# Attention with a fused dense layer on one core: the first maxima lead the scores by 32 instead of 48, their relu gets two places per side, and the next rows' statistics stand two by two ahead of two maxima

## The reference

```python
xn = layernorm(x)
q = relu(xn @ Wq.T + bq); k = relu(keys @ Wk.T + bk); v = relu(values @ Wv.T + bv)
# 16 heads of 16 columns
score = einsum('bhsd,bhtd->bhst', qh, kh) / sqrt(16)
attn = softmax(score, axis=-1)
a = transpose(einsum('bhst,bhtd->bhsd', attn, vh), (0, 1, 3, 2)).reshape(...)
w = (weights >= 0) * 2 - 1
y = clip((xn @ w.T) * scale + bias, -100, 100)
out = x + (a + xn) + y
```

## Time and profile before

| | us |
|---|---|
| median of 3 runs (2899.27 to 2910.23) | 2900.64 |
| profiled execution | 2900.54 |
| its span, first to last instruction | 2898.7 |
| TensorE busy, 97% of the span | 2809.6 |
| ScalarE busy, 84% | 2439.8 |
| VectorE busy, 81% | 2341.8 |
| GpSimd busy, 32% | 938.2 |
| mean granted TensorE clock, of full speed | 0.981 |

### The profile page before, as it was taken

The page is one execution under the profiler, slowest core; times in us unless marked ns, Lnnn a source line. Parts: engine busy times, 40 slices in busy tenths (PEclk is TensorE's granted clock), DMA queues, the critical chain, the costliest instruction groups (busy, mean ns, idle before and its releaser), DMA issues.

```text
span 2898.7 us, 61156 instructions
## 1 busy us (share of the span) xinstructions
PE 2809.6 (97%) x17860; PEld 1195.3 (41%) x17860; DVE 2341.8 (81%) x4578; ACT 2439.8 (84%) x2955; POOL 938.2 (32%) x845
## 2 busy tenths in 40 slices
PE   8899999999999999999999999999999999999996
PEld 4444444444444434444444444444444444444331
DVE  6788888888888888888888888888888888888840
ACT  4788888888888888888888888888888888888896
POOL 4304333242343314433242342414333242343001
PEclk8599999999999999999999999999999999999998
DMA  7111111121211111111111211121111121211111
GB/s 140 58 38 55 64 62 35 61 65 58 64 62 50 46 65 58 64 60 37 61 64 58 64 59 49 50 68 54 64 62 35 61 65 57 64 62 36 46 54 38
DMA packets 78637, 167.75 MB, mean 58 GB/s; under 512 B 28547, under 2 KB 32646, under 8 KB 76326
## 3 DMA queue, kind: packets, MB, share of 16 engines
q1 hardware_dynamic: 78374, 164.19, 18.8%
HBM read 36.71 MB, written 17.83 MB: 19 GB/s over the span
## 4 chain that ended last, share of the span: by engine, by line
PE 73%; issue 11%; DVE 7%; ACT 3%; POOL 1%; DVEq 0%; SPq 0%; DMA 0%; ACTq 0%; POOLq 0%
PE value_ps L606 27%; PE ring L628 24%; PE score_ps L592 16%; DVE mx L950 6%; ACT probs L798 3%; PE score_ps L657 1%; PE score_ps L672 1%; PE score_ps L674 1%; PE score_ps L659 1%; PE score_ps L661 1%; POOL fin L1088 1%; DVE stats L975 1%; DVE excess L926 0%; DVEq L945 0%; PE ring L637 0%
## 5 line engine op out<-in xcount | busy, mean ns | idle before, releaser
L798 ACT ACTIVATE probs<-score_ps 128x1024 f32<-128x1024 f32 x2048 | 1996.6, 1027 | 301.0 <-PE score_ps L592 292.6
L950 DVE TENSOR_REDUCE mx<-ring 128x1 f32<-128x512 f32 x2940 | 1894.0, 684 | 348.0 <-PE ring L628 335.3
L628 PE MATMUL ring<-kstack,qstack 48*128 48x512 f32 x3430 | 1125.0, 464 | 11.1 <-DVE mx L950 4.5
L606 PE MATMUL value_ps<-probs,vones 128*32 128x512 f32 x8192 | 1093.3, 606 | 0.8 <-ACT probs L798 0.3
L628 PEld LDWEIGHTS ring<-kstack,qstack 48*128 48x128 f32 x3430 | 525.5, 184 | 948.3 <-DVE mx L950 891.8
L592 PE MATMUL score_ps<-qstack,kstack 51*128 51x512 f32 x4096 | 827.0, 426 | 24.3 <-ACT probs L798 15.5
L592 PEld LDWEIGHTS score_ps<-qstack,kstack 51*128 51x128 f32 x4096 | 414.1, 186 | 262.6 <-ACT probs L798 222.2
L1088 POOL TENSOR_TENSOR dense<-dense,affine 128x512 f32<-128x512 f32 x128 | 164.1, 1282 | 869.6 <-ACT dense L848 868.2
L926 DVE CUSTOM_DVE_ANT_0 excess<-ring,excess 128x512 f32<-128x512 f32 x534 | 369.2, 691 | 78.0 <-PE ring L628 49.9
L814 ACT ACTIVATE excess<-ring 128x512 f32<-128x512 f32 x490 | 293.9, 600 | 7.6 <-PE ring L628 4.4
L606 PEld LDWEIGHTS value_ps<-probs,vones 128*32 128x32 f32 x8192 | 161.5, 108 | 288.3 <-issue 276.6
(11 more groups left out here) (93 smaller groups left out, 1437.0 us busy)
## 6 DMA issues: line engine op xcount, KB each, us to landing
qstack<-parts SPq DMA_DIRECT2D x768, 64.0 KB, 2.5
fin<-taken SPq DMA_DIRECT2D x256, 128.0 KB, 2.9
xin<-x SPq DMA_DIRECT2D x16, 1024.0 KB, 4.9
base_cur<-base_new SPq DMA_DIRECT2D x16, 1024.0 KB, 5.4
fin<-recip SPq DMA_DIRECT2D x32, 512.0 KB
out<-fin SPq DMA_DIRECT2D x32, 512.0 KB, 2.6
qstack<-proj SPq DMA_DIRECT2D x256, 12.0 KB
kstack<-base_cur SPq DMA_DIRECT2D x16, 128.0 KB, 6.2
```

What stands on the lines that cost most here:

```text
L606: mm = pe.matmul(value_ps[h4 * 32:(h4 + 1) * 32, :], vones[:, 2 * tp + c, hh * HALF + side * PAIRS + 2 * g + j, :, :], probs[:, q % 2 * GR ...
L628: pe.matmul(ps[:, :], qstack[nh][rows, pair, st * P:(st + 1) * P], keys, start=True, stop=True).then_inc(s_mm, 1)
L798: nc.scalar.activation(probs[:, q % 2 * GROUP + u % GROUP, :], score_ps[src][:, :], ACT.Exp, scale=EXP_SCALE).then_inc(s_probs, 1)
L950: nc.vector.tensor_reduce(most, src[:, :], AX.X, ALU.max).then_inc(s_mx, 1)
```

## The change

`LEAD` goes from 48 to 32. The start has 40 steps instead of 44. In each pass the next half's maxima, and the splits with them, begin at duo 24 instead of 20, and `ROWS_DUO` goes from 22 to 26. The relu of the start has two places for each side, chosen by the parity of the step, and waits for the join of the step before the last. The start's statistics stand in steps 35 to 38, its aggregates behind step 39, which is now the last. In the passes the statistics stand in the duos 15, 17, 19 and 21, one ahead of maximum 3 and one ahead of maximum 6 of the octet. On SyncE gather 2 stands ahead of the load of the rows.

```diff
-        start_excess = [excess[:, :], probs[:, 4, 0:BANK]]
+        start_excess = [[excess[:, :], probs[:, 4, 0:BANK]], [probs[:, 5, k * BANK:(k + 1) * BANK] for k in range(2)]]
...
-        LEAD = 48
-        ROWS_DUO = 22
+        LEAD = 32
+        ROWS_DUO = 26
         RECIP_UNIT = 14
         AGGREGATE_DUO = 23
+
+        STATS_DUOS, STATS_AHEAD = (15, 17, 19, 21), (3, 6)
...
-        START_STATS = FIRST_ROWS + 5
-        assert START_ROWS < len(START)
+        START_STATS = FIRST_ROWS + 3
+        assert max(START_ROWS, START_STATS + 4) < len(START)
...
+                if att:
+                    gather(*att, 2)
                 if now:
                     load_rows(b, hh)
-                if att:
-                    gather(*att, 2)
...
             def take_start_differences(j):
                 for side in range(SIDES):
-                    wait(act, s_mx, 2 * (j - 1) + side + 1)
+                    wait(act, s_mx, 2 * (j - 2) + side + 1)
                     act.wait_ge(s_mm, 2 * SIDES * j + side + 1)
-                    nc.scalar.activation(start_excess[side], score_ps[j % 2][:, side * BANK:(side + 1) * BANK],
+                    nc.scalar.activation(start_excess[j % 2][side], score_ps[j % 2][:, side * BANK:(side + 1) * BANK],
...
-                    join(ring[at[side]][:, :], start_excess[side], mx[:, hh, st, h, 1:2])
+                    join(ring[at[side]][:, :], start_excess[j % 2][side], mx[:, hh, st, h, 1:2])
...
                         for n in itertools.chain(*maxima_of(d)):
+                            if prep and d in STATS_DUOS and n % 8 in STATS_AHEAD:
+                                statistics(b, *ROW_TILES[2 * STATS_DUOS.index(d) + STATS_AHEAD.index(n % 8)])
                             reduce_bank(b, hh, n, at)
...
-                    if prep and AGGREGATE_DUO - 8 <= d < AGGREGATE_DUO:
-                        statistics(b, *ROW_TILES[d - AGGREGATE_DUO + 8])
```

## The result

| | before | changed kernel |
|---|---|---|
| median, us | 2901.32 (20 runs, 2897.91 to 2910.23) | 2913.36 (20 runs, 2906.0 to 2926.04) |
| ratio, 95% interval | | 1.0038 [1.0029, 1.0048] |
| profiled execution / its span, us | 2900.5 / 2898.7 | 2911.5 / 2909.7 |
| mean granted TensorE clock | 0.981 | 0.978 |

The forecast was 2880 us, its range 2869 to 2891. The kernel became slower, clear of the interval but by less than the 0.5% that the prediction named as its bound for a change.

What follows compares the result with a forecast made beforehand. TensorE and VectorE were taken to hold each other in the long middle, with VectorE idling in gaps. From 2900.5 us: start -9.5, last pass +1.8, statistics -10.2, queries -3.4, rows +1 gave 2880 us, range 2869 to 2891.

Steps and rivals of the forecast that it cites:

- The start, -9.5 us: Before the first pass: steps go from 1.50 to 1.24 us, GpSimd's root starts at 106.1 for 116.13; -9.5 us.
- Rival (a): In the start: steps stay in the relu and join loop, giving -3.8 for -9.5, total 2886 us; chance 0.14.
- The last pass, +1.8: Last pass with maxima: duos 20 to 23 get maxima and take 9.8 us for 8.0; +1.8 us.
- The statistics, -10.2: In 14 hh=0 passes: moved statistics use VectorE's gaps, their extra 1.43 us becomes 0.7; -10.2 us.
- The 0.1 us a pair: hh=0 passes: allowance for a 0.33 us statistic exceeding the gap ahead of the join; 0.4 us over the pairs.
- Rival (b): In passes with statistics: the statistics keep their price, term 0, total 2890 us; chance 0.15.
- rival (c): In hh=0 passes: statistics and aggregates become free, 1.43 becomes 0.2, 7 us less, total 2873 us; chance 0.12.
- the 1.43: Extra us six pairs take in hh=0 over hh=1, for statistics, aggregates and their effect on the maxima's splits.
- The flush: On VectorE: a 0.42 us statistic would hold the engine about 0.57 us, making the statistics term 0, sum about 2890.
- The queries, -3.4: Next half's queries: one 1.75 us TensorE wait and the 3.4 us at half clock after it go; -3.4 us.
- The rows, +1: Rows turned at duo 26 in 31 passes: ScalarE's copy near the sums and splits costs 0.03 us each; +1 us.
- rival (d): Rows' load lands too late for the next pass's scores, margin 2.2 us; 2926 us if held 3.7 us; chance 0.04.

Runs made afterwards that it cites:

- experiment 1: Changed kernel with 32 waiting instructions ahead of TensorE's first work, putting its loop head back at 1750: 2867.95 us, ratio to before 0.9887.
- experiment 7: Kernel before with only the statistics of the passes moved, loop head staying at 1750: 2889.47 us, ratio 0.9960.
- experiments 11 and 12: Kernel of experiment 1 with 18 waiting instructions more on ScalarE, then also 24 on VectorE: 2871.72 us and 2873.67 us.
- experiment 9: Kernel before with only the two relu places per side in the start: 2888.33 us, ratio 0.9962.
- experiment 2: Kernel before with 224 waiting instructions ahead of TensorE's first work, loop head at 1974: 2963.94 us, ratio 1.0215.
- experiment 3: Changed kernel with the same 32 waiting instructions put behind the last pass instead: 2913.95 us, ratio to before 1.0046.

## Why the prediction was wrong, step by step

- **The start, -9.5 us:** right. Pass 1 begins 9.5 us earlier in the changed kernel and 10.2 in the kernel of experiment 1; root at 105.97, predicted 106.1; steps of 1.22 us, predicted 1.24. That root is what counts holds: the first exponential came 12.0 us earlier, and 2.5 us of that were given back in pass 0, in the stall on the normalised rows. Rival (a) fell.
- **The last pass, +1.8:** measured +1.5. The four duos take 9.9 us with their maxima, predicted 9.8, for 8.00:

```profile
2794.25:2804.15 9.90, 9.83 (x67) 3.77 (x63) 9.13 (x17) 8.61 (x12) 0.00 (x0) 1.00 0.00 0
```

- **The statistics, -10.2:** direction right, too small. In the kernel without stops a pass with hh = 0 is 1.07 us shorter, -15 us for 14 passes. Alone the statistics give -0.76 (experiment 7) and the lead -0.08. The 0.1 us a pair that I kept for a statistic in a gap of 0.24 is not there, the pairs take 4.88 us. The last 0.2 us comes only with both moves together; that it lies in the splits beside the aggregates is not shown. Rival (b) fell, and rival (c) was nearer than the forecast: it left 0.2 us of the 1.43, the runs 0.36. The flush that the prediction sets against this term is not in the changed kernel either: the join starts 0.33 us after a statistic of 0.41 (430.67). The section of the Trainium skill that the prediction cites for it (VectorE: DVE Perf Modes, the DRAIN you can't avoid) also says that a next operation that is not held starts earlier, which the prediction leaves out: so the section does not speak against this term as the prediction has it.
- **The queries, -3.4:** right in the mechanism, and in the size by luck of the execution. Pass 10 is 3.3 us shorter, but it is so too in the three other traces with a lead of 48. One of these, experiment 9's, has a wait of 1.66 us in pass 26 and one of 0.47 in pass 30, one (experiment 7's) a wait of 0.40 in pass 30, and one (experiment 2's) 0.13 in pass 30. No trace with the lead of 32 has any. So the wait is an event that moves and can be absent, and by those three traces the term is worth some 2 us or less.
- **The rows, +1, and rival (d):** nothing. The load is issued from 453.69 for 6.05 us, 6.18 in the earlier trace rows, and TensorE's first scores of the next pass wait for no DMA. The passes with hh = 1, which carry the move as well, are as long as before (in the median 85.49 before, 85.45 changed), and 85.37 in experiment 1.
- **What failed** is the step that dealt with the four steps taken out of the start. The prediction said that they come back at the end for +1.8 us, and it costed them as time only: VectorE's joins at one end, two pairs of duos at the other. They are also 32 instructions of TensorE's program, and the sum had no term for where the program's loop then lies. That missing term is +41 us: 13 stops of 1.9 to 2.5 us, and five stretches at half clock. None of the four rivals contained it. The prediction's own test, "the forecast is wrong as a whole if the hh=1 passes lengthen", looked at the wrong half: these have no jump ahead of them.
- **A second missing term**, -3.9 us in pass 29, has the same nature on ScalarE and VectorE (experiments 11 and 12). The kernel before has its other stretch at half clock there, 3.4 us from 2691.0, behind ScalarE's stop; the prediction, which named the one in pass 10 only, did not see it.
- With these terms the sum comes out: 2880.2, less 0.3 for the last pass, 4.4 for the statistics (14 x 1.04 beside 10.2, against the 87.06 from which the stops are counted), 1.3 for the rows and 3.9 in pass 29, plus 0.1 for the queries and 41.0 for the stops, is 2911.4, for 2911.5 in the profiled execution.
- **Without the stops** the forecast would have been 12 us too high: experiment 1 measured 2867.95, just under the range. What it missed there is 4.8 us of the statistics, 4.3 in pass 29 and 2.4 in the passes with hh = 1, where the rows were to cost 1 us and the time fell by 1.4; the rest is in small parts.

The version to keep is the kernel of experiment 1: the whole change, with the head of TensorE's loop where it was. It is 1.1% faster than the kernel before, and its runs lie within 0.35 us of each other where those of before spread over 12.

## What to carry to other kernels

An edit ahead of a loop moves the loop in every engine's program, and a loop whose head lay 16 or fewer instructions ahead of a block's border (one such distance was tried) paid some 2 us at each jump here, and often the clock after it; one whose head lay some 50 ahead paid too. Before believing the verdict on such an edit, compare the packets of the instruction queues on the two pages (172 and 185 here) and look for "issue" waits of 2 us in the middle of runs of equal instructions. If they are there, move the head by some waiting instructions and time again: the ratio of this change turned from 1.0038 [1.0029, 1.0048] to 0.9887 [0.9872, 0.9903].

## What the runs showed of the hardware

- TensorE's program comes in packets of 16384 bytes; a block that came behind a jump had landed 2.2 to 2.8 us after the branch (at 550.18: packet at +1.2 us, 1.2 us long), and the next matmul started only 1.2 to 1.5 us later (554.03 for 552.6); what these are stays open. The hint saves 3.7 us of idle time at a jump (4.10 - 0.39), and covers one block.
- ScalarE's and VectorE's come in packets of 8192 bytes, and the first pass behind a loop cost ScalarE a stop of 2.15 us and VectorE one of 2.20 us in two kernels that differ from a third only by 18 and 24 instructions that do nothing.
- A stop of TensorE of 2 us was followed by the half clock five times of 13 in the changed kernel, four in experiment 3 and eleven in experiment 2, for 3.4 to 10.2 us; in the kernel before a wait of 1.75 us had done the same.
- A semaphore that is named as releaser can be innocent: ScalarE's 2.15 us were put down to VectorE.
